# Two neighbouring scans as one of 1024 columns, in both scan phases of a two-layer selective-scan kernel; two products per unit move from GpSimd to VectorE

## What is computed

```python
# layer 0; layer 1 has the same recurrence
delta = softplus(dts + dt_projs_bias)
A = -exp(A_logs)
def step(h, inp):
    dl, ul, bl, cl = inp
    h = exp(dl[..., None] * A) * h + (dl * ul)[..., None] * bl[:, :, None, :]
    y = einsum('bkdn,bkn->bkd', h, cl)
    return h, y
ys = ys + Ds * u
```

## Time and profile before

| | |
|---|---|
| time, median of 3 runs | 29,964.53 us (29,957.32 to 29,972.79) |
| profiled execution | 29,961.96 us, its span 29,960.2 us |
| TensorE (PE) busy | 23,943.2 us, 80% |
| VectorE (DVE) busy | 26,267.2 us, 88% |
| ScalarE (ACT) busy | 16,148.3 us, 54% |
| GpSimd (POOL) busy | 25,221.1 us, 84% |
| scans, L868 | 15,296 records, 18,631.7 us |
| VectorE's products, L878 | 5,632, 6,384.4 us |
| dbu, L806 | 5,634, 17,614.3 us |
| GpSimd's products, L815 | 4,864, 6,123.9 us |
| decays, L733 | 15,360, 10,435.9 us |

### The profile page before, as it was taken

The page is one execution under the profiler, slowest core; times in us unless marked ns, Lnnn a source line. Parts: engine busy times, 40 slices in busy tenths (PEclk is TensorE's granted clock), DMA queues, the critical chain, the costliest instruction groups (busy, mean ns, idle before and its releaser), DMA issues. The chain is left out here.

```text
span 29960.2 us, 220709 instructions
## 1 busy us (share of the span) xinstructions
PE 23943.2 (80%) x56446; PEld 9042.9 (30%) x56446; DVE 26267.2 (88%) x22439; ACT 16148.3 (54%) x26407; POOL 25221.1 (84%) x11112
## 2 busy tenths in 40 slices
PE   8777777777777777777777777776689988888887
PEld 3222222222222222222222222222234433333322
DVE  8899999999999999999999999998531189999984
ACT  2455555555555555555555555555222266666652
POOL 1699999999999999999999999998200089999972
PEclk9999999999999999999999999999889999999998
DMA  6433333333333333333333333333632267777765
GB/s 209 172 134 133 131 134 133 134 132 131 134 133 130 135 133 133 134 131 134 133 131 134 133 134 132 131 134 141 226 120 76 72 227 229 230 231 230 230 215 184
DMA packets 1243378, 4581.47 MB, mean 153 GB/s; under 512 B 254416, under 2 KB 292320, under 8 KB 876768
## 3 DMA queue, kind: packets, MB, share of 16 engines
q1 hardware_dynamic: 1136208, 4218.14, 40.2%
q10 hardware_dynamic: 105904, 349.22, 3.3%
HBM read 3908.27 MB, written 658.64 MB: 152 GB/s over the span
## 5 line engine op out<-in xcount | busy, mean ns | idle before, releaser
L868 DVE TENSOR_TENSOR_SCAN s_h<-s_dA,s_state,s_dbu 128x512 f32<-128x512 f32 x15296 | 18631.7, 1273 | 257.8 <-ACT s_dA L733 246.3
L806 POOL TENSOR_TENSOR s_dbu<-s_du,s_b_sb 128x1536 f32<-128x1536 f32 (+1 forms) x5634 | 17614.3, 3132 | 4.8 <-DVE s_h L868 2.9
L733 ACT ACTIVATE s_dA<-s_delta,s_negA 128x512 f32<-128x512 f32 x15360 | 10435.9, 687 | 8328.7 <-DVE s_h L868 8319.1
L607 PE MATMUL s_y_ps<-s_hc,s_ident 128*128 128x512 f32 x20992 | 10042.0, 597 | 1.5 <-DVE s_hc L878 1.5
L878 DVE TENSOR_TENSOR s_hc<-s_h,s_c_ps 128x1024 f32<-128x1024 f32 (+1 forms) x5632 | 6384.4, 1134 | 428.0 <-issue 406.6
L815 POOL TENSOR_TENSOR s_hc_pool<-s_h,s_c_sb 128x512 f32<-128x512 f32 x4864 | 6123.9, 1259 | 204.9 <-DVE s_h L868 200.6
L597 PE MATMUL s_c_ps<-s_bc,s_sel 96*128 96x512 bf16 x6400 | 2360.9, 388 | 3937.2 <-DVE s_hc L878 3936.3
L615 PE MATMUL s_y_ps<-s_hc_pool,s_ident 128*128 128x512 f32 x9728 | 5025.7, 598 | 0.0
L607 PEld LDWEIGHTS s_y_ps<-s_hc,s_ident 128*128 128x128 f32 x20992 | 4048.8, 193 | 2966.2 <-issue 2756.9
L823 POOL TENSOR_TENSOR s_du<-s_delta,s_u 128x1536 f32<-128x1536 f32 (+1 forms) x450 | 1125.1, 2500 | 2115.3 <-ACT s_delta L720 2071.1
L597 PEld LDWEIGHTS s_c_ps<-s_bc,s_sel 96*128 96x128 bf16 x6400 | 573.8, 97 | 7615.4 <-DVE s_hc L878 6576.6
(11 more groups left out here) (142 smaller groups left out, 14187.5 us busy)
## 6 DMA issues: line engine op xcount, KB each, us to landing
s_b_sb<-rows SPq DMA_DIRECT2D x1794, 1024.0 KB, 5.1
s_c_sb<-rows SPq DMA_DIRECT2D x1216, 1024.0 KB, 6.7
s_u<-U SPq DMA_DIRECT2D x257, 768.0 KB
Y<-s_yo ACTq DMA_DIRECT2D x256, 768.0 KB, 8.4
m_y<-Y SPq DMA_DIRECT2D x192, 1024.0 KB, 7.5
s_u<-U SPq DMA_DIRECT2D x193, 256.0 KB
U<-f_row SPq DMA_DIRECT2D x24, 2048.0 KB, 17.3
U<-f_col SPq DMA_DIRECT2D x24, 2048.0 KB, 7.1
```

The lines of the kernel that those rows point to most:

```text
L607: last = pe.matmul(y_ps[:, t, :], ident[:, :], hc[:, s % 2, j, :], start=False, stop=nd > 1 and s == NS - 1)
L733: act.activation(dA[:, n % DECAYS, :], delta[g % 2][:, t, :], ACT.Exp, scale=negA[g % 2][:, a:a + 1]).then_inc(dA_ready, 1)
L806: pool.tensor_tensor(dbu[:, s % AHEAD, :, :], a, b, ALU.mult).then_inc(dbu_ready, 1)
L868: dve.tensor_tensor_scan(h[:, s % (2 * GROUP), j, :], dA[:, (n * J + j) % DECAYS, :], dbu[:, s % AHEAD, j, :], initial, ALU.mult, ALU.add) ...
```

## The change

Tiles 0 and 1 of a step are scanned by one instruction of 1024 columns. `SCANS` says which tiles a scan takes: in layer 0 tiles (0, 1) and then tile 2, in layer 1 the one scan of both. For the recurrence to begin anew at column 512, the decay of that column is a zero that is written into every bank once, at the start (`dA[:, :, 0:1]`); the decay of tile 1 then leaves that column out (511 columns). What the initial value would have added there, first_dA * state, ScalarE adds to dbu of that column, in a new instruction of one column, `carry`, after the decay of tile 1; it waits for dbu, and the merged scan waits for it (`carried`). `first_dA`, the decay of the first position for all 16 states, is one activation of 16 columns behind softplus. The first unit has no carry. A decay of tile 0 or 1 waits for the merged scan that last read its bank.

In layer 0 steps 5 and 11 leave `SHARE`: VectorE forms the product of all three tiles there, 1536 columns, and GpSimd none. The rows of C for GpSimd are loaded as before (`C_STATES`).

```diff
 
-    SHARE = tuple(range(NS)) if nd > 1 else (0, 2, 4, 6)
+    C_STATES = tuple(range(NS)) if nd > 1 else (0, 2, 4, 6)
+    SHARE = tuple(s for s in C_STATES if nd == 1 or s not in (5, 11))
     NSH = len(SHARE)
...
     B_RING = 2 if nd > 1 else 4
-    C_PARTS = NSH // ROWS_IN
-    C_STEP = ng * (SHARE[1] - SHARE[0])
+    C_PARTS = len(C_STATES) // ROWS_IN
+    C_STEP = ng * (C_STATES[1] - C_STATES[0])
 
...
     on_pool = dict(du=11 if nd > 1 else 7)
+
+    SCANS = ((0, 1),) if nd == 1 else ((0, 1), (2,))
+    SC = len(SCANS)
+    MERGED = SCANS[0] == (0, 1)
+    FIRST_ROW, FIRST_TILE = divmod(1, nd)
+
+    def scans_to(k, j):
+
+        return k * SC + [j in tiles for tiles in SCANS].index(True) + 1
 
...
                 n = g * C_PARTS + part
-                wait(eng, hcp_ready, (n - 1) * ROWS_IN)
+                if n >= 2:
+                    last = C_STATES[(n - 2) % C_PARTS * ROWS_IN + ROWS_IN - 1]
+                    wait(eng, hcp_ready, pool_products((n - 2) // C_PARTS, last))
                 first = N_STATE + ng - 1 + part * ROWS_IN * C_STEP
...
                 act.preload_act_table_set("natural_log_exp_and_others")
+                if MERGED:
+                    act.wait_ge(delta_ready, g + 1)
+                    act.wait_ge(negA_ready, g * 3 + 2)
+                    act.activation(first_dA[q][:, :], negA[q][:, FIRST_TILE * N_STATE:(FIRST_TILE + 1) * N_STATE], ACT.Exp,
+                                   scale=delta[q][:, FIRST_TILE, 0:1]).then_inc(first_dA_ready, 1)
+
+            def carry(g, s):
+
+                n = g * NS + s
+                act.wait_ge(dbu_ready, n + 1)
+                act.wait_ge(first_dA_ready, g + 1)
+                act.wait_ge(state_saved, (g - 1) * GROUPS + s // GROUP + 1)
+                a = s * ng + FIRST_ROW
+                first = dbu[:, s % AHEAD, 1, 0:1]
+                act.activation(first, state[:, s, 1:2], ACT.Identity, scale=first_dA[g % 2][:, a:a + 1],
+                               bias=first).then_inc(carried, 1)
 
...
                     act.wait_ge(negA_ready, g * 3 + 3)
-                wait(act, scanned, n - DECAYS + 1)
+                if n >= DECAYS:
+                    act.wait_ge(scanned, scans_to((n - DECAYS) // J, (n - DECAYS) % J))
                 a = t * N_STATE + s * ng + r
-                act.activation(dA[:, n % DECAYS, :], delta[g % 2][:, t, :], ACT.Exp,
+                skip = 1 if MERGED and j == 1 else 0
+                act.activation(dA[:, n % DECAYS, skip:], delta[g % 2][:, t, skip:], ACT.Exp,
                                scale=negA[g % 2][:, a:a + 1]).then_inc(dA_ready, 1)
 
             def save_states(g, i):
 
-                act.wait_ge(scanned, (g * NS + (i + 1) * GROUP) * J)
+                act.wait_ge(scanned, (g * NS + (i + 1) * GROUP) * SC)
                 slots = slice(i % 2 * GROUP, (i % 2 + 1) * GROUP)
...
                         decay(g, s, j)
+                        if MERGED and j == 1 and g:
+                            carry(g, s)
                     if s == on_act["evacuate"] and g:
...
                 m = pool_products(g, s) - 1
-                part = m // ROWS_IN
-                pool.wait_ge(scanned, (g * NS + s + 1) * J)
+                row = C_STATES.index(s)
+                part = g * C_PARTS + row // ROWS_IN
+                pool.wait_ge(scanned, (g * NS + s + 1) * SC)
                 pool.wait_ge(c_in[part % 2], (part // 2 + 1) * 16)
                 wait(pool, summed_pool, m - 3)
                 pool.tensor_tensor(hc_pool[:, m % 4, :], h[:, s % (2 * GROUP), J - 1, :],
-                                   c_sb[:, part % 2, m % ROWS_IN, :], ALU.mult).then_inc(hcp_ready, 1)
+                                   c_sb[:, part % 2, row % ROWS_IN, :], ALU.mult).then_inc(hcp_ready, 1)
 
...
             dve.tensor_copy(sel[:, :, :].rearrange("p a b -> p (a b)"), self32).then_inc(sel_ready, 1)
+            dve.memset(dA[:, :, 0:1], 0.0).then_inc(column_zero, 1)
             dve.memset(minus[:, :, :], 0.0).then_inc(minus_set, 1)
...
 
-            def scan(g, s, j):
+            def scan(g, s, i):
                 n = g * NS + s
-                if j == 0:
+                tiles = SCANS[i]
+                j, end = tiles[0], tiles[-1] + 1
+                if i == 0:
                     dve.wait_ge(dbu_ready, n + 1)
...
                         wait(dve, state_saved, g * GROUPS + s // GROUP - 1)
-                dve.wait_ge(dA_ready, n * J + j + 1)
+                    if MERGED and g:
+                        dve.wait_ge(carried, n - NS + 1)
+                dve.wait_ge(dA_ready, n * J + end)
                 initial = state[:, s, j:j + 1] if g else 0.0
-                dve.tensor_tensor_scan(h[:, s % (2 * GROUP), j, :], dA[:, (n * J + j) % DECAYS, :],
-                                       dbu[:, s % AHEAD, j, :], initial, ALU.mult, ALU.add).then_inc(scanned, 1)
+                bank = (n * J + j) % DECAYS
+                dve.tensor_tensor_scan(h[:, s % (2 * GROUP), j:end, :].rearrange("p a j -> p (a j)"),
+                                       dA[:, bank:bank + end - j, :].rearrange("p a j -> p (a j)"),
+                                       dbu[:, s % AHEAD, j:end, :].rearrange("p a j -> p (a j)"),
+                                       initial, ALU.mult, ALU.add).then_inc(scanned, 1)
 
             def times_c(g, s):
                 n = g * NS + s
                 own = in_product(s)
-                dve.wait_ge(scanned, n * J + own)
+                dve.wait_ge(scanned, scans_to(n, own - 1))
                 dve.wait_ge(c_done, n + 1)
...
                 for s in range(NS):
-                    for j in range(J):
-                        scan(g, s, j)
-                        if j == 0 and g * NS + s:
+                    for i in range(SC):
+                        scan(g, s, i)
+                        if i == 0 and g * NS + s:
                             times_c((g * NS + s - 1) // NS, (s - 1) % NS)
```

More of the change, by code:

```diff
@@ L435, in scan_phase @@
         state = sb("state", [128, NS, J])
+        first_dA = [sb(f"first_dA{q}", [128, N_STATE]) for q in range(2)]
         ident = sb("ident", [128, 128])
@@ L458, in scan_phase @@
         D_ready, direct_done = sem("D_ready"), sem("direct_done")
+        column_zero, first_dA_ready, carried = sem("column_zero"), sem("first_dA_ready"), sem("carried")
         OWN = nd - 1 if nd > 1 else nd
@@ L776, in _ @@
             act.wait_ge(sel_ready, 1)
+            act.wait_ge(column_zero, 1)
             take_xproj(0)
@@ L802, in input_of @@
                     pool.wait_ge(du_ready, g + 1)
-                wait(pool, scanned, (n - AHEAD + 1) * J)
+                wait(pool, scanned, (n - AHEAD + 1) * SC)
                 a, b = du[g % 2][:, :, :], b_sb[:, s % (B_RING * STEPS_IN), :, :]
```

## The result

| | predicted | measured |
|---|---|---|
| time after | 29,815 us (29,600 to 30,120) | 30,185.62 us, median of 4 runs (30,182.05 to 30,187.88) |
| time before, in the same comparison | | 29,966.99 us, median of 4 runs (29,957.32 to 29,972.79) |
| after / before | 0.995 | 1.0073 (95% interval 1.0056 to 1.0091) |
| unit of layer 0 | 76.3 us | 77.62 us (before 77.18) |
| unit of layer 1 | 26.15 us | 26.29 us (before 25.75) |

A forecast was written before the change was run, and what follows sets the result against it. GpSimd sets layer 0's pace at 77.18 us a unit; VectorE has no gap in layer 1. Layer 0 -225 and layer 1 +77 us sum to -148, from 29,961.96, 2.6 under the runs' median, to 29,815 us (29,600 to 30,120).

The forecast's parts named there:

- term 5: Layer 0, start of a unit: scan 2 stops 0.2 us, the 1.7 at step 1 goes; unit 76.3, -225 us.
- Term 1: Scans on VectorE: each merge saves 0.113 us, 1.81 a unit in layer 0; bounds 0.06 and 0.19.
- Term 2: Layer 0, steps 5 and 11: the products add 1.07 us a unit on VectorE; GpSimd falls to 74.72.
- Term 3: Ordinary layer 0 step on ScalarE: the carry takes 0.38 us, and the step hides it with slack 0.4.
- Term 4: Layer 0, step 8: behind softplus the merged scan stops 2.31 us, against 1.00 before.
- Term 6: Layer 1: stops of 0.74 us at scan 3 and 0.65 at scan 5; unit 26.15, +77 us.
- B: Rival: x projection still at 1.2 GHz in most units, 1.70 us a unit at scan 2; 30,250 us; chance 0.17.
- A: Rival: ScalarE stays hidden everywhere, layer 0 at GpSimd's 74.72 us, layer 1 at 24.8; 29,150 us; chance 0.06.
- C: Rival: a merge saves less, 0.075 us for 0.113; 29,970 us, no change; chance 0.11.
- D: Rival: the carry delays merged scans by more than the slack of 0.4 in every step; about 30,300 us; chance 0.05.
- The "issue" stop: Layer 0, step 1: VectorE's stop of 1.7 us, from the x projection waiting for its loads, goes.
- the three signs of being wrong: Stops at other steps than 2, 8 (layer 0) or 3, 5 (layer 1); merged scans 2.45; x projection 4.4 in most units.

The follow-up runs named there:

- fill: The changed kernel with four matmuls that nobody reads added on TensorE in step 14 of each layer 0 unit; 29,852.4 us.
- ln0_s59: The changed kernel with states 5 and 9 moved, not 11, and layer 0's softplus as logarithm of 1 + exp without table loads; 29,452.4 us.
- move_only: The changed kernel with the old unmerged scans in both layers, the two products still moved; 29,800.8 us.
- s59_l1un: The changed kernel with the products of states 5 and 9 moved, not 11, and the old unmerged scans in layer 1; 29,760.0 us.

## Why the prediction was wrong

**The step that failed is in term 5: "PE then needs 0.06 and 2.9 for a C broadcast, two sums and the pool's sum".** The 2.9 was read off a stretch at full clock. I used the clock for the x projection, and looked at what the missing load would do to it; I did not ask what the moved product leaves on TensorE three steps later. Its pool sum is 0.86 of work from start to start, and without it the idle time of step 14 is 1.58 + 0.86 = 2.44. Term 5 laid out from D, the start of merged scan 15 at 10020.71:

| from D | forecast | trace |
|---|---|---|
| C broadcast, then sums | 3.51 | 3.49 |
| x projection starts | 6.41 | 7.99 |
| C broadcast of step 0 | 9.08 | 10.57 |
| evacuation | 11.21 | 12.71 |
| next decay | 12.13 | 13.62 |
| scan 2 (due 13.65) | 13.86 | 15.45 |
| stop | 0.2 | 1.80 |

Every link but one held within 0.1. 4.50 stood where 2.9 did, 1.6 too much, and it came in 200 units of 256. From fill, the price is 333 us; the forecast with it is 29,815 + 333 = 30,148, 38 us short of what was measured.

**The other terms.** Term 1: taken as 0.113 a merge, a merged scan of 2.25; measured 2.24 to 2.26. In layer 0 all 16 shorten VectorE's work, but most of it went into the longer stop at step 8: the merge returned 54 us net. Term 2: a product of 1536 columns takes 1.64 against 1.11, 0.53 as said, and GpSimd's 74.72 is the 74.74 of ln0_s59. Term 3: carry 0.373 (forecast 0.38); ordinary steps repeat every 4.55 with no stop. From the carry's end to the scan are 0.22 or 0.23, not the 0.13 taken from a decay, which lowers the slack to 0.3 and puts 0.1 on each stop. Term 4: forecast 2.31, measured 66.41 - 63.99 = 2.42, that 0.1. Term 6: forecast 0.74 and 0.65, measured 0.79 and 0.61; the mean unit is 0.14 over the forecast, of which 8 x 0.01 are the scans, 27 us in all.

**The rivals.** B had the right sum, 30,250 against 30,186, and the right kind: work on TensorE at 1.2 GHz at a unit's turn, its delay at scan 2, in most units (0.78 of them). It had the wrong instructions. It slowed the x projection, which ran at 2.74; the sums ahead of it were slow. I gave it 0.17, because TensorE "will have idled hardly at all right before" the x projection. That was true, and beside the point: the idling came one piece earlier. A is refuted by the two ScalarE stops, C by 2.26, D by 4.55. The "issue" stop is gone, as forecast. The range ended at 30,120 since it took B in up to seven units of ten; the slow clock came in nearly eight of ten, at some 1.7 each as B has it, and layer 1 adds 27 us: the range missed by 66. Of the three signs of being wrong that the prediction names, none came true. No step stops but 2 and 8 in layer 0 and 3 and 5 in layer 1, a merged scan lasts 2.35, and the x projection takes 2.74: they watched the wrong instructions on TensorE as well.

**Taken apart.** Moving two products gains 166 us (move_only). Merging in layer 0 adds 54 by the units, where the clock holds (76.53 to 76.32; s59_l1un is 41 below move_only). Merging in layer 1 costs 92. The lowered clock costs 333. -166 - 54 + 92 + 333 = +205, of the 219 measured.

**Open.** Why 56 of the 256 units escape, about every fourth or fifth. TensorE's timeline of such a unit (the rows from 5190) and of the next (from 5266), in the profile after:

```profile
5190.18 2.74 PE L621 MATMUL s_y_ps<-s_hc,s_ident 128*128 128x512 f32 x6
...
5203.60 0.39 PE L611 MATMUL s_c_ps<-s_bc,s_sel 96*128 96x512 bf16 x1 [2.44 <-DVE s_hc L922]
5203.82 1.88 PE L621 MATMUL s_y_ps<-s_hc,s_ident 128*128 128x512 f32 x4
...
5266.58 4.44 PE L621 MATMUL s_y_ps<-s_hc,s_ident 128*128 128x512 f32 x6
...
5280.22 3.41 PE L621 MATMUL s_y_ps<-s_hc,s_ident 128*128 128x512 f32 x4
```

The spared unit idles the same 2.44, and its sums run at full clock. One thing differs: in the unit that stops, the three sums over the product of state 11, which TensorE makes in step 12, took 4.44, slow as well, 13 us ahead of the turn; in the spared one they took 2.74. The same 4.44 stands ahead of the turn shown from 10024 on (it starts at 10010.79). Over the 251 units with complete rows, both places are slow in 187, neither in 54, and only the turn in 10. So the clock of a turn goes with the clock of step 12 in nearly all units, and what decides which of the two patterns a unit falls into is not settled. Nothing was run on it.
